# Attention and Mamba2 layers on one core: the time-step columns share the gate's projection, and eleven steps of the schedule move

## What is computed

```python
# layer 0, n = 4096 tokens, D = 32, C = 256
q, k = wq @ xf + bq, wk @ xf + bk             # 1x1 convolutions
attn = softmax(einsum('bnd,bdm->bnm', q, k))
v = wv @ xf + bv
x = gamma * einsum('bcn,bmn->bcm', v, attn) + x
# layer 1, on u = layernorm(x over channels) * norm_g + norm_b
z, xBC, dt = split(u @ in_w.T)                # 256, 512 and 4 columns
dt = softplus(dt + dt_bias)                   # 4 heads
xBC = silu(causal depthwise conv of 4 taps (xBC) + conv_b)
xs, Bm, Cm = split(xBC)                       # 256, 128, 128
state = state * exp(dt * A) + dt * xs (x) Bm  # scan over 4096 tokens
y = (Cm . state + Dp * xs) * silu(z)
out = (y * rsqrt(mean(y*y) + eps) * rms_w) @ out_w.T
gate = sigmoid(relu(mean(out over tokens) @ se1_w.T + se1_b) @ se2_w.T + se2_b)
result = x + out * gate
```

## Time and profile before

| | |
|---|---|
| median of 3 runs | 3153.75 us (3151.14 to 3154.02) |
| the profiled execution | 3150.87 us |
| its span | 3148.7 us |
| granted clock of PE, mean | 0.983 |
| PE busy | 2980.0 us, 95% of the span, 21208 instructions |
| DVE busy | 2032.0 us, 65%, 3417 instructions |
| POOL busy | 2009.9 us, 64%, 3087 instructions |
| ACT busy | 1930.0 us, 61%, 3742 instructions |

### The profile page before, as it was taken

How to read it: one execution, slowest core, us unless ns; L and a number is a source line. 1 busy time by engine, 2 the same in 40 slices (tenths; PEclk the granted TensorE clock), 3 DMA queues, 4 the chain that set the end, 5 groups by cost and what they waited for, 6 DMA issues and landing times. The chain is left out here.

```text
span 3148.7 us, 63156 instructions
## 1 busy us (share of the span) xinstructions
PE 2980.0 (95%) x21208; PEld 2322.5 (74%) x21208; DVE 2032.0 (65%) x3417; ACT 1930.0 (61%) x3742; POOL 2009.9 (64%) x3087
## 2 busy tenths in 40 slices
PE   6899999999999999999999999999999999999984
PEld 3767777777777777777777777777777777777762
DVE  5556666666666676676676666676666667666654
ACT  2565666666656566666665666666666666666652
POOL 2446666667756576666676656666676667777753
PEclk9999999999999999999999999999999999999986
DMA  3111111111311121222221222122221111212121
GB/s 123 49 37 46 44 51 58 31 54 49 103 63 65 58 71 58 91 77 74 82 77 38 72 76 72 62 76 69 65 89 36 43 49 55 69 50 69 42 95 67
DMA packets 101970, 200.99 MB, mean 64 GB/s; under 512 B 18480, under 2 KB 41392, under 8 KB 97264
## 3 DMA queue, kind: packets, MB, share of 16 engines
q1 hardware_dynamic: 98192, 195.08, 18.6%
q10 hardware_dynamic: 3456, 1.86, 0.2%
HBM read 131.21 MB, written 64.75 MB: 62 GB/s over the span
## 5 line engine op out<-in xcount | busy, mean ns | idle before, releaser
L723 POOL TENSOR_TENSOR p_lo<-p,p_hi 128x512 f16<-128x512 f32 x1024 | 1221.9, 1201 | 845.6 <-ACT p_hi L886 711.9
L879 ACT ACTIVATE p<-p_et 128x512 f32<-128x512 f32 x1024 | 612.2, 598 | 637.4 <-PE p_et L1138 598.0
L1156 PE MATMUL acc<-v_hi,p_hi 128*128 128x257 f16 x4096 | 954.3, 273 | 4.0 <-DVE work L1464 3.8
L1158 PE MATMUL acc<-v_lo,p_hi 128*128 128x256 f16 x4096 | 951.8, 272 | 0.0
L1420 DVE TENSOR_REDUCE maxes<-p_mx 128x1 f32<-128x1024 f32 x508 | 620.1, 1221 | 489.1 <-PE p_mx L1117 488.7
L886 ACT ACTIVATE p_hi<-p 128x512 f16<-128x512 f32 x1024 | 643.5, 629 | 10.0
L1164 PE MATMUL acc<-v_hi,p_lo 128*128 128x257 f16 x4096 | 622.8, 274 | 15.1 <-POOL p_lo L723 15.1
L1156 PEld LDWEIGHTS acc<-v_hi,p_hi 128*128 128x128 f16 x4096 | 399.3, 97 | 125.0 <-issue 54.8
L1158 PEld LDWEIGHTS acc<-v_lo,p_hi 128*128 128x128 f16 x4096 | 400.6, 98 | 117.8 <-issue 49.9
L1164 PEld LDWEIGHTS acc<-v_hi,p_lo 128*128 128x128 f16 x4096 | 399.9, 98 | 68.0 <-POOL p_lo L723 15.9
L1138 PE MATMUL p_et<-qs,kst 98*128 98x256 f16 x2048 | 393.3, 273 | 11.6 <-ACT p L879 11.1
(11 more groups left out here) (213 smaller groups left out, 4164.2 us busy)
## 6 DMA issues: line engine op xcount, KB each, us to landing
work<-rows_d SPq DMA_DIRECT2D x32, 1024.0 KB, 5.2
xin<-in_x_dram SPq DMA_DIRECT2D x48, 512.0 KB, 4.7
xr<-in_x_dram SPq DMA_DIRECT2D x32, 512.0 KB, 3.8
x_d<-x1c SPq DMA_DIRECT2D x31, 512.0 KB, 2.9
og_d<-og SPq DMA_DIRECT2D x29, 512.0 KB, 2.7
mix_x<-x_d SPq DMA_DIRECT2D x25, 512.0 KB, 4.7
mix_o<-og_d SPq DMA_DIRECT2D x24, 512.0 KB, 5.5
out_dram<-mix_o SPq DMA_DIRECT2D x24, 512.0 KB, 2.8
```

Of the source, the lines that this page charges most:

```text
L723: e.tensor_tensor(p_lo[:, n % RING, :], p32[:, n % P32S, :], p_hi[:, n % RING, :], ALU.subtract).then_inc(lo_pool, 1)
L879: e.activation(p32[:, n % P32S, :], p_et[:, :], ACT.Exp).then_inc(exp_done, 1)
L1156: e.matmul(acc[:, t, 0:C + 1], p_hi[:, r, at:at + P], v_hi[:, 2 * k + kk, 0:C + 1], start=(k == 0 and kk == 0), stop=False)
L1158: e.matmul(acc[:, t, 0:C], p_hi[:, r, at:at + P], v_lo[:, 2 * k + kk, :], start=False, stop=False, skip_group_check=True)
```

## The change

- dt has no fill of its own. Each 128-token tile of a block has one fill of 260 columns: 256 of z and 4 of dt. So z has four fills a block (steps 10, 11, 13, 15) in place of two (22, 24), with four tanh on ACT and four products on DVE, and DVE adds the bias of dt in four pieces. The projection's weights lie in two buffers now, loaded by two more DMAs on ACT's queue at the start, and `zt` has a second buffer, so that a block's gate can be written while the last block's is read.
- Softplus of dt starts five steps later: its DVE pieces at 15 and 17 (were 10 and 12), its POOL parts at 18 to 21 (were 13 to 16). The decays' exponential, transpose and running sum stand at 24, 25 and 27 (were 19, 21 and 23), with the DMAs that carry the decays' rows to DRAM and back at 27.
- The first xsB fill stands at 26 (was 25), x1's transposes at 3 (were at 2), the second xT fill of the residual at 19 (was 30), with its load on SP at 20.
- `max_parts` stands ahead of stage b's and stage a's pieces in DVE's step.

The diff, cut (of the table one line; the numbers of the others are above; the old dt fill and the old DVE block stood where lines are gone):

```diff
-K_X1T, K_UT, K_DT, K_DAT, K_CUM, K_YT, K_OUT = 2, 9, 10, 21, 23, 30, 0
+K_X1T, K_UT, K_DT, K_DAT, K_CUM, K_YT, K_OUT = 3, 9, 15, 25, 27, 30, 0
...
-        inT_sb = sb("inT_sb", [P, CH, 2 * C + 2 * NST + NH])
+        inT_sb = sb("inT_sb", [P, CH, CONVD])
+        inz_sb = sb("inz_sb", [P, CH, C + NH])
...
+        zt = [zt0, sb("zt1", [P, QT, C])]
...
-                e.wait_ge(zs_done, 2 * g + 2)
+                e.wait_ge(zs_done, QT * g + c + 1)
...
-                if K == K_DAT - 2:
+                if K == K_DAT - 1:
                     e.wait_ge(dt_ready, g + 1)
...
-                for r in range(2):
-                    if K == K_Z[r]:
-                        key = ("z", g, r)
+                for t in range(QT):
+                    if K == K_Z[t]:
+                        key = ("z", g, t)
                         e.wait_ge(filled, n_filled(key))
-                        wait(e, y_ready, g * QT)
-                        e.activation(zt[:, 2 * r:2 * r + 2, :], bank(key)[:, :].rearrange("p (t c) -> p t c", t=2),
-                                     ACT.Tanh, scale=0.5).then_inc(ztanh_done, 1)
+                        wait(e, y_ready, (g - 1) * QT)
+                        e.activation(zt[g % 2][:, t, :], bank(key)[:, 0:C], ACT.Tanh, scale=0.5).then_inc(ztanh_done, 1)
...
-                elif name == "dt":
+                elif name == "z":
                     e.wait_ge(uT_done, 2 * g + 2)
                     o = begin(key)
-                    for t in range(QT):
-                        for h in range(CH):
-                            mm = e.matmul(o[:, t * NH:(t + 1) * NH], uT[:, h, t * P:(t + 1) * P],
-                                          inT_sb[:, h, C + CONVD:C + CONVD + NH], start=(h == 0), stop=(h == CH - 1))
-                    mm.then_inc(filled, 1)
-                elif name == "z":
-                    o = begin(key)
-                    for t in range(2):
-                        for h in range(CH):
-                            mm = e.matmul(o[:, t * C:(t + 1) * C], uT[:, h, (2 * i + t) * P:(2 * i + t + 1) * P],
-                                          inT_sb[:, h, 0:C], start=(h == 0), stop=(h == CH - 1))
+                    for h in range(CH):
+                        mm = e.matmul(o[:, 0:C + NH], uT[:, h, i * P:(i + 1) * P], inz_sb[:, h, :],
+                                      start=(h == 0), stop=(h == CH - 1))
                     mm.then_inc(filled, 1)
...
+                for t in range(QT):
+                    if K == K_Z[t]:
+                        key = ("z", g, t)
+                        e.wait_ge(ztanh_done, QT * g + t + 1)
+                        if t == 0:
+                            wait(e, dt_ready, g)
+                        v.tensor_tensor(dtt[:, 0, t * NH:(t + 1) * NH], bank(key)[:, C:C + NH], dtb[:, :], ALU.add)
+                        v.scalar_tensor_tensor(zt[g % 2][:, t, :], zt[g % 2][:, t, :], 1.0, bank(key)[:, 0:C],
+                                               ALU.add, ALU.mult).then_inc(zs_done, 1)
+                if K == K_DT:
...
+                    if K % STEPS == (K_PARTS if n >= STEPS else K_PARTS_FIRST) and n // STEPS + 1 < NHALF:
+                        max_parts(n // STEPS + 1)
```

More of the change, by code:

```diff
@@ L59 @@
 K_SQ = (8, 12, 16, 21)
-K_XT = (13, 30)
+K_XT = (13, 19)
 K_XB = 4
@@ L130, in fills_at @@
             out += [("uT", A, 0), ("uT", A, 1)]
-        if K == K_DT:
-            out += [("dt", A, 0)]
         if K == K_DAT:
@@ L136, in fills_at @@
             out += [("cumT", A, 0)]
-        for r in range(2):
-            if K == K_Z[r]:
-                out += [("z", A, r)]
+        for t in range(QT):
+            if K == K_Z[t]:
+                out += [("z", A, t)]
         for c in range(QT):
@@ L268, in conv_attention_mamba_kernel @@
         yT = work[:, 4096:5120].rearrange("p (h n) -> p h n", h=CH)
-        zt = work[:, 5120:6144].rearrange("p (t c) -> p t c", t=QT)
+        zt0 = work[:, 5120:6144].rearrange("p (t c) -> p t c", t=QT)
         dAb = work[:, 6144:8192]
+        zt = [zt0, sb("zt1", [P, QT, C])]
         xin = [sb(f"xin{r}", [P, CH, BLK]) for r in range(2)]
@@ L397, in conv_attention_mamba_kernel @@
         uT_done = sem("uT_done")
-        dtin_done = sem("dtin_done")
         dtabs_ready = sem("dtabs_ready")
@@ L480, in emptied @@
                 "out": (og_done, 2 * g + i + 1), "x1T": (x1c_done, 2 * g + i + 1),
-                "uT": (uT_done, 2 * g + i + 1), "dt": (dtin_done, g + 1), "dAT": (dAr_done, g + 1),
-                "cumT": (cum16_done, g + 1), "z": (zs_done, 2 * g + i + 1), "xsB": (xsB_done, QT * g + i + 1),
+                "uT": (uT_done, 2 * g + i + 1), "dAT": (dAr_done, g + 1),
+                "cumT": (cum16_done, g + 1), "z": (zs_done, QT * g + i + 1), "xsB": (xsB_done, QT * g + i + 1),
                 "cb": (mt_ready, QT * g + i + 1), "y": (yt_ready, QT * g + i + 1), "st": (S_ready, QT * g + i + 1),
@@ L928, in stage_a @@
                         e.wait_ge(filled, n_filled(key))
-                        wait(e, filled, n_filled(("z", g - 1, 1)) if g else 0)
+                        wait(e, filled, n_filled(("z", g - 1, QT - 1)) if g else 0)
                         e.activation(uT[:, h, :], bank(key)[:, :], ACT.Identity, bias=bcol[:, h:h + 1],
@@ L1276, in convolve @@
                 for h in range(CH):
-                    mm = e.matmul(conv_bank(g, m), inT_sb[:, h, C + m * P:C + (m + 1) * P], uT[:, h, :],
+                    mm = e.matmul(conv_bank(g, m), inT_sb[:, h, m * P:(m + 1) * P], uT[:, h, :],
                                   start=(h == 0), stop=(h == CH - 1))
@@ L1531, in stage_a @@
                         v.memset(xbc[:, :, 0:HALO], 0.0).then_inc(halo_done, 1)
-                for r in range(2):
-                    if K == K_Z[r]:
-                        key = ("z", g, r)
-                        e.wait_ge(ztanh_done, 2 * g + r + 1)
-                        v.scalar_tensor_tensor(zt[:, 2 * r:2 * r + 2, :], zt[:, 2 * r:2 * r + 2, :], 1.0,
-                                               bank(key)[:, :].rearrange("p (t c) -> p t c", t=2), ALU.add, ALU.mult)\
-                            .then_inc(zs_done, 1)
+                for t in range(QT):
+                    if K == K_Z[t]:
+                        key = ("z", g, t)
[6 more added lines that the diff above has]
+                if K == K_DT:
+                    e.drain()
+                    v.scalar_tensor_tensor(dtt[:, 1, :], dtt[:, 0, :], -1.0, dtt[:, 0, :], ALU.mult, ALU.max)\
+                        .then_inc(dtabs_ready, 1)
+                    v.tensor_scalar(dtt[:, 3, :], dtt[:, 0, :], 0.0, None, ALU.max)
+                if K == K_DT + 2:
+                    e.wait_ge(dtexp_done, g + 1)
+                    v.tensor_scalar(dtt[:, 4, :], dtt[:, 2, :], 2.0, None, ALU.add)
+                    e.drain()
+                    v.reciprocal(dtt[:, 5, :], dtt[:, 4, :])
+                    e.drain()
+                    v.tensor_tensor(dtt[:, 4, :], dtt[:, 2, :], dtt[:, 5, :], ALU.mult).then_inc(dtz_ready, 1)
                 if K == K_DAT:
@@ L1634, in step @@
                 if s < G:
-                    if K % STEPS == (K_PARTS if n >= STEPS else K_PARTS_FIRST) and n // STEPS + 1 < NHALF:
-                        max_parts(n // STEPS + 1)
                     if K == K_BN:
```

30 lines of the change are left out of this document (6 added, 24 removed).

## The result

The changed kernel takes **3170.45 us** (median of 5 runs, 3167.51 to 3175.78) beside 3153.21 for the kernel before (5 runs, 3148.49 to 3154.02): a ratio of 1.0062, 95% interval 1.0048 to 1.0075. It is slower by 17 us, where the forecast was 3141, faster. The profiled execution's span is 3173.7 us, 25.0 longer than before's 3148.7.

What follows compares the result with a forecast made beforehand. PE was taken as the bound, busy 2852.58 of 2936.00 us. Per slot -2.24 us and +1.7 given back make -0.54, -16.7 over 31 slots; with +4 in the tail the forecast is 3141 us, range 3100 to 3178.

Steps and rivals of the forecast that it cites:

- PE's own work: PE's matmuls: dt's fill goes and z's fills get 4 columns wider, -1.65 us a slot, 512 instructions fewer.
- The sign that was given for it: In the profile after the change, PE's busy time was to be down by some 58 us.
- the two waits that go: PE's waits at the first cb fill (0.25 us a slot) and the second xT fill (0.34 us) disappear.
- the new ones: New waits of PE at PSUM banks and for ACT, DVE and POOL give back +1.7 us a slot.
- the second xsB fill: Step 27: PE waits for ACT's xsB eviction, 0.8 us a slot (0.25 to 1.4), some 25 us in all.
- the cb fill behind z's third tile: Step 14: the fourth cb fill waits for DVE's z product, 0.45 us a slot (0 to 0.75), some 14 us.
- x1T's term: x1's transposes at step 3 wait for the second cb product's bank (step 6): 0.15 us a slot.
- POOL's chain: From PE's start of step 18 (T): outputs, softplus, `p_lo`, then Newton steps from T + 14.1 to 18.4; hardly later than before.
- Rival D: POOL's chain from step 18 becomes the bound, taps and `p_lo` slowing each other: 3160 to 3191 us, slower; chance 0.19.
- The step that failed: DVE's step 6: `max_parts` ahead delays one cb product by its four instructions, 0.1 us a slot.
- The tail: Last block: all of softplus stands between output and Newton steps, so yT starts later: +4 us (0 to 6).

Runs made afterwards that it cites:

- run 11: Changed kernel with the split of the maxima back behind and only the second mr fill of a slot moved from step 24 to 25: 3117.7 us, ratio 0.9896.
- run 3: Changed kernel with only POOL's Newton steps one step later (24 instead of 23): 3195.3 us, ratio 1.0139.
- run 2: Changed kernel with the split of the maxima back behind stage b's and stage a's pieces in both of its steps: 3135.9 us, ratio 0.9949.
- 6: Changed kernel with the split of the maxima first only in step 22, behind the other pieces in step 6: 3172.1 us, ratio 1.0069.
- 7: Changed kernel with the split of the maxima first only in step 6, behind the other pieces in step 22: 3143.6 us, ratio 0.9977.
- run 5: Kernel before with only the split of the maxima ahead of stage b's and stage a's pieces in DVE's step: 3166.6 us, ratio 1.0047.
- The two small moves: x1's transposes at 3 and residual's second fill at 19, alone on the kernel before: 3138.2 us; undone on run 2: 3176.2 us.
- run 13: Changed kernel, split of the maxima still first, with the third channel group's convolution at step 20 instead of 21: 3163.9 us, ratio 1.0041.

## Why the prediction was wrong, by its own steps

**PE's own work: right.** -1.65 us in 31 slots is -51; the trace has -47.5 once the clock is taken out, with 512 instructions fewer. The z fills of 260 columns take 134.3 us busy, 11.4 more than before, and dt's 60.8 us are gone. The sign that was given for it, busy time down by some 58 us, did not show: it is down by 20.5 (2980.0 to 2959.5), since at the lower clock the same work is busy for longer.

**The size of the waits: near, by luck; their places: wrong.** The steps gave -0.59 for the two waits that go and +1.7 for the new ones, in 31 slots +34 us of idle time; it is +37.4. But they were to be at the second xsB fill (25 us) and at the cb fill behind z's third tile (14 us). At the xsB fills ACT is waited for once, for 1.0 us (and three times, 5.7 us in all, DVE's query rows are); z's product is waited for at the cb fills three times, for 3.8 us. Only x1T's term stood: 4.7 forecast, 5.1 measured, in four places. The largest term, 0.8 us a slot at the second xsB fill, had a slip besides: 20.3 less 3.46 and 0.33, plus 0.44, is 16.9 and not 16.7, which makes that wait 0.5 us. No run here shows it: even in run 11, where PE is held least, ACT's xsB is waited for 1.7 us in all. What came in its place is the 46.3 us at the exponential of step 26.

**POOL's chain: right, and not what mattered.** In slot 24 step 18 begins at 2391.55 and the Newton steps at 2406.28:

```profile
2391.55 0.38 PE L1138 MATMUL p_et<-qs,kst 98*128 98x256 f16 x2
```

```profile
2406.28 0.20 POOL L762 TENSOR_TENSOR rw<-rw 128x4 f32<-128x4 f32 x1 [0.35 <-DVE rw L1469]
```

That is T + 14.7; the working had 14.1. Rival D rested on this chain and on POOL being slowed by DVE. POOL's `p_lo` takes 1187 ns in the mean, not more than before (1201). The collision is there, and goes the other way: DVE's small instructions wait for POOL's `p_lo`. D took its 1.41 us from a `p_lo` at 2547.64 "beside DVE's taps", but the taps had ended at 2547.38; beside it DVE ran two instructions with both tensor inputs in SBUF:

```profile
2547.29 2.31 DVE L1600 SCALAR_TENSOR_TENSOR mix_o<-mix_o,gate,mix_x 128x512 f32<-128x512 f32 x2
```

A tap has one of its two tensor inputs in PSUM, and the rule that D drew on (the Trainium skill, "SBUF — State Buffer", section "Who interferes with whom") speaks of two inputs in SBUF. The trace agrees: a tap takes 755 ns in the mean where a `p_lo` runs beside it, and 755 ns where none does. The time, 3170, lies in D's range, but run 3 shows that D is not the reason.

**The step that failed** is the one on the split of the maxima, "`max_parts` ahead in step 6 delays one cb product by its four instructions: 0.1". It priced the move in step 6 and left out step 22, where the same four instructions go ahead of three taps, a tanh and an exponential, in the very steps from which z's 3.5 us of matmuls had gone. The working did use that loss of cover, but only for POOL's chain, not for DVE's. Runs 2, 6 and 7 give the price: 34 us for the move, or 1.1 us a slot where the working had 0.1, nearly all at step 22. Where z's matmuls still stand between steps 22 and 24 the same move costs 13 us (run 5); the other 21 come with the lost cover. Without the move the time is 3135.9, 5 us from the forecast, but that too is no proof of the working: 39.0 us of waits at the mr fill are in it, which no term had.

**The clock: no term.** The prediction took 1.00 for the long stretch, and every microsecond of waiting at a microsecond. 11 falls behind waits of 1.9 to 3.1 us at step 26 lose 23.9 us, the four others 15.4; the kernel before loses 13.7 in its five, which makes the +25.5 us. Leaving the clock out, the stretch is 10.1 us shorter than before (-47.5 + 37.4) and the tail 6.1 us longer (below): nearly even. The clock makes it a clear loss.

**The tail: half right.** The forecast had yT's transposes 4 us later against the last silu. The last silu is at 3090.12 in the changed kernel, so they begin 15.2 us behind it, before 11.1: +4.1. Against the last exponential it is 66.5 us, before 61.8: +4.7.

```profile
3105.35 1.94 PE L1171 MATMUL pl<-ident,work 128*128 128x128 f32 x8 [0.36 <-ACT xsB L965]
```

Most of the other 4.8 us come right behind it: from yT's first transpose over the output projection to the next cb fill are 8.93 us (3105.35 to 3114.28), before 5.52 (3085.16 to 3090.68). That stretch ran at full clock before, and mostly at half now. The 11 us from yT on, in the changed kernel and in the kernel before:

```profile
3106.00:3117.00 11.00, 9.66 (x29) 5.29 (x27) 2.12 (x3) 2.75 (x6) 2.33 (x4) 0.66 0.08 32
```

```profile
3085.00:3096.00 11.00, 8.10 (x34) 4.84 (x34) 3.40 (x6) 3.04 (x8) 3.89 (x6) 1.00 0.00 0
```

The +3.4 us fit what the clock can have cost, at most 0.34 x 11 = 3.7 us. So without the clock the tail is some 6.1 us longer than before, not 9.5, of which 4.7 are ahead of yT and 1.4 behind the output projection, where no run places them.

**Open** is what makes half of the 13 us that the split first costs on the kernel before. The two small moves are worth 40 us on one kernel and 15 on the other, in the profiled executions 45.2 and 12.3. The clock makes most of that difference: on the one the moves gain 11.9 us of it, on the other they lose 8.5, which is 20.4 of 32.9 us; idle time makes 8.2 and the tail 4.6. Why the clock goes one way here and the other way there stays open.

## What to carry to other kernels

Work that leaves a stretch of a busy engine was also the cover of every chain that ran beside it. Before it is moved, measure each of those chains (here DVE's maxima, split, taps, then ACT's tanh and exponential), not only the one on the engine that gets more work, and leave the room that it needs: one fill moved by one step turned 3135.9 us into 3117.7. On a kernel whose PE is at 97%, a stall of two microseconds is priced by what the clock does after it, too: here waits 37.4 us longer brought 25.5 us of lost clock with them.

## What was not expected of the hardware

- Small instructions of DVE between SBUF operands stretch to the length of the POOL instruction beside them: 0.17 us becomes 0.97 to 1.15 beside a `p_lo` of 1.14, one small instruction for each `p_lo` in a row (two of them in slot 20 of the changed kernel, three in run 3). The taps, which add into PSUM, took 1.59 us for two beside a `p_lo` in run 2, as they do elsewhere.
- A fall of the clock costs 1.7, 3.4 or 5.1 us, in no other sizes, in all the kernels here up to the last exponential; it came behind PE's idle time of two microseconds in some slots, and not in others with the same 1.99 us. In run 13 eighteen waits at step 26 of 1.3 us had no fall behind them; the one fall at step 26 came behind a wait of 2.01 us.
